# Two-layer adaLN attention kernel: 2-head exponentials in layer 0, ScalarE normalisation, and the small parts spread over each row

## The reference, cut to what matters

```python
h = layernorm(x) * (1 + ca) + sa          # "P" norm of the kernel
# layer 0: 16 heads of 8, plus one rotary part of 32 shared by all heads, causal
scores = einsum(q, k) + einsum(q_rope, k_rope)[:, None];  scores /= sqrt(40)
w = softmax(where(causal, -inf, scores));  x += ga * ((w @ v) @ W_o)
h = layernorm(x) * (1 + cb) + sb          # "T" norm
# layer 0: one shared and 15 routed experts, all computed, top 3 gated
x += gb * (shared(h) + sum_e gate_e * expert_e(h) + h)
# layer 1: the same frame; grouped qkv, 16 heads of 8, no mask
# layer 1 feed-forward: 8 experts, top 1, after one more layernorm of h ("I" norm)
```

## Time and profile before

| | us |
|---|---|
| median of 3 runs | 984.2 (981.91 to 987.36) |
| the profiled execution | 984.84 |
| its span, first to last instruction | 983.1 |
| TensorE busy | 792.4 (81%) |
| VectorE busy | 649.1 (66%) |
| ScalarE busy | 524.2 (53%) |
| GpSimd busy | 344.6 (35%) |

### The profile page before, as it was taken

How to read it: one execution, slowest core, us unless ns; L and a number is a source line. 1 busy time by engine, 2 the same in 40 slices (tenths; PEclk the granted TensorE clock), 3 DMA queues, 4 the chain that set the end, 5 groups by cost and what they waited for, 6 DMA issues and landing times. The chain is left out here.

```text
span 983.1 us, 12967 instructions
## 1 busy us (share of the span) xinstructions
PE 792.4 (81%) x4212; PEld 497.0 (51%) x4212; DVE 649.1 (66%) x1290; ACT 524.2 (53%) x970; POOL 344.6 (35%) x389
## 2 busy tenths in 40 slices
PE   3547888988898889999989899789989888527850
PEld 2233444555454667787767544345344444227740
DVE  3135568676663777776768696488898876347853
ACT  1013454545556677776757456456656656217740
POOL 3413775543532000000005345653453542133425
PEclk9987999999999999999999979899999999659985
DMA  4251331102110490000002112210110200011013
GB/s 125 48 95 21 85 81 35 34 22 46 30 24 2 137 285 6 1 1 1 1 8 57 43 42 63 60 35 17 38 25 18 58 4 10 4 54 56 32 34 84
DMA packets 56414, 44.75 MB, mean 46 GB/s; under 512 B 6598, under 2 KB 47387, under 8 KB 56347
## 3 DMA queue, kind: packets, MB, share of 16 engines
q1 hardware_dynamic: 55323, 41.82, 16.8%
q0 software_dynamic: 1024, 2.10, 0.7%
HBM read 14.67 MB, written 14.55 MB: 30 GB/s over the span
## 5 line engine op out<-in xcount | busy, mean ns | idle before, releaser
L926 ACT ACTIVATE ring<-single 128x512 f32<-128x512 f32 (+3 forms) x512 | 253.1, 517 | 226.3 <-PE single L1176 218.8
L1554 DVE TENSOR_REDUCE mneg<-pair 128x2 f32<-128x1024 f32 (+3 forms) x256 | 258.5, 1022 | 87.7 <-PE pair L1160 33.2
L1176 PE MATMUL single<-q_op,k_op 104*128 104x512 f32 (+3 forms) x512 | 216.5, 443 | 17.8 <-ACT ring L926 9.2
L1156 PE MATMUL pair<-k_op,q_op 96*128 96x512 f32 (+3 forms) x512 | 172.1, 415 | 42.2 <-DVE mneg L1554 22.6
L786 POOL TENSOR_SCALAR k_op<-k_stk,cst 104x512 fp32r<-104x512 f32 x64 | 100.0, 1577 | 276.2 <-DMA k_stk<-hl 258.5
L1176 PEld LDWEIGHTS single<-q_op,k_op 122*128 122x128 f32 (+1 forms) x512 | 97.9, 197 | 98.6 <-ACT ring L926 72.6
L1156 PEld LDWEIGHTS pair<-k_op,q_op 120*128 120x128 f32 (+1 forms) x512 | 98.9, 207 | 86.8 <-DVE mneg L1554 44.8
L1192 PE MATMUL p_o<-ring,vaug 128*9 128x512 f32 (+3 forms) x1024 | 116.1, 526 | 1.0 <-ACT ring L926 0.9
L721 POOL TENSOR_SCALAR_AFFINE_SELECT ring<-ring 128x256 f32<-128x256 f32 x128 | 52.3, 408 | 149.4 <-ACT ring L926 149.2
L955 ACT ACTIVATE ring<-pair,cols 128x512 f32<-128x512 f32 x136 | 86.1, 685 | 33.8 <-PE pair L1236 27.5
L1600 DVE TENSOR_TENSOR ring<-ring,single 128x1024 f32<-128x1024 f32 x60 | 73.3, 1221 | 45.5 <-ACT ring L955 44.4
(11 more groups left out here) (294 smaller groups left out, 1306.4 us busy)
## 6 DMA issues: line engine op xcount, KB each, us to landing
xs<-zero SPq DMA_DIRECT2D x10, 1024.0 KB, 10.1
q_op<-hl SPq DMA_DIRECT2D x96, 64.0 KB, 2.0
stage<-in_L_ffn_W_dram SPq DMA_DIRECT2D x8, 512.0 KB, 4.5
stage<-in_L_ffn_rW_dram SPq DMA_DIRECT2D x6, 512.0 KB, 5.1
k_op<-hl SPq DMA_DIRECT2D x48, 64.0 KB
k_stk<-hl SPq DMA_DIRECT2D x48, 64.0 KB, 2.0
xb<-xs SPq DMA_DIRECT2D x15, 128.0 KB, 2.0
xs<-yb SPq DMA_DIRECT2D x15, 128.0 KB, 1.7
```

Source lines behind the costliest of these rows:

```text
L926: exp_done.by(act.activation(ring[:, n % 8, lo:T], singles[n % 2][:, lo:T], ACT.Exp), (L, n))
L1156: ins = pe.matmul(both[:, i, 0:hi], r32(qs[:, P * qt:P * (qt + 1)]), r32(ks[:, 0:hi]), start=i == 0 or L == 1 or qt >= 2, stop=L == 1)
L1176: st_full.by(pe.matmul(singles[n % 2][:, lo:T], r32(ks[:, P * kc:P * (kc + 1)]), r32(qs[:, lo:T]), start=True, stop=True), (L, n))
L1554: s_taken.by(dve.tensor_reduce(mneg[:, G % 2, 2 * p:2 * p + 2, qt], both[:, :, 0:hi], axis=AX.X, op=ALU.max, negate=True), (L, m))
```

## The change

1. **Layer 0's exponentials two heads wide.** Layer 0 swaps its PSUM tiles: an exponential covers two heads (2 x 512 down to 2 x 128) in a `pair` tile, so a quad has two of them, and `max_unit` uses `single`: head pairs for query tiles 0 and 1, single heads for 2 and 3, twelve units for each group in place of eight.
2. **The parts spread over all quads** in both tables. Layer 0's `P.rs` moves from quad 4 to quad 7, the `mt` parts from "b" to "d" of quads 2, 6, 10, 14, and `rt2` and `gt` of a row come two rows later (`U.`). SyncE's list in layer 0 is not edited.
3. **The P norms of rows 1 to 3 together** (`BATCH`, new function `batch`): statistics of three rows, then one chain of Newton steps on 128x12 numbers, beside quads 0 to 3 of each layer's first row.
4. **Normalised rows by ScalarE** (`P.ne`, `T.ne`, `he`): four ACTIVATE with a pointer for bias and for scale, 128x128 each, in place of four on VectorE, which now computes only the shift (`norm_shift`).
5. **Layer 1's weight splits two to a row**, after the masks, and SyncE's loads for them at the end of the row.

```diff
-        spread = (((-5, (0, 1, 2)), (-4, (3, 4, 5)), (-3, (6, 7))), ((-6, (0, 1)), ...
+        spread = (((-5, range(0, 4)), (-4, range(4, 7)), (-3, range(7, 10)), (-2, range(10, 12))),
...
-          (2, "b"): ["mt1", "P.ne"], (2, "d"): ["T.proj"], (3, "b"): ["P.ln1", "T.ns"], (3, "d"): ["P.rp", "T.na"],
-          (4, "b"): ["T.n1"], (4, "d"): ["P.rs", "T.n2"], (5, "b"): ["ot0", "T.n3"], (5, "d"): ["P.q"],
-          (6, "b"): ["mt2", "T.ne"], (6, "d"): ["P.k"], (7, "b"): ["P.v"], (7, "d"): ["T.ln2"],
+          (4, "d"): ["P.ln1"], (5, "b"): ["ot0"], (5, "d"): ["P.rp"], (6, "b"): ["P.q"], (6, "d"): ["mt2", "T.na"], (7, "b"): ["P.rs"],
+          (8, "b"): ["P.k"], (8, "d"): ["T.n1"], (9, "b"): ["ot1", "T.n2"], (9, "d"): ["P.v"], (10, "b"): ["T.n3"], (10, "d"): ["mt3", "T.ne"],
...
+BATCH = {(0, "b"): "B.s1", (0, "d"): "B.s2", (1, "b"): "B.s3", (1, "d"): "B.sd", (2, "b"): "B.n1", (2, "d"): "B.n2", (3, "b"): "B.n3"}
...
 # SyncE, layer 1
                 m_dma(1, G + 1)
-                if r == 0:
-                    expert1(2)
-                    expert1(3)
                 m_dma(1, G + 2)
...
+                    expert1(2 * r + 2)
+                    expert1(2 * r + 3)
 # ScalarE
+                if name == "P.ne":
+                    normed.wait_ge(act, ("B.n3", L) if r else key)
...
+                    for t in range(NT):
+                        shift, scale = norm_of("P", s, t)
+                        ins = act.activation(xn[:, t, :], x[:, r, t, :], ACT.Identity, bias=shift, scale=scale)
+                    xn_ready.by(ins, key)
...
+                    at = 2 * (n % 4)
+                    ins = act.activation(ring[:, at:at + 2, lo:T], pairs[n % 2][:, :, lo:T], ACT.Exp)
 # TensorE, layer 0's quad
+                        exp_unit(L, Q, 0)
+                        for m in waiting[0:2]:
+                            max_unit(L, m)
+                        exp_unit(L, Q, 1)
+                        for name, b in beside_quad(s, q, "b"):
+                            part(name, b)
+                        for m in waiting[2:]:
+                            max_unit(L, m)
+                        if Q:
+                            values(L, Q - 1)
```

More of the change, by code:

```diff
@@ L931, in attention @@
                     Q = 4 * NG * (s % NB) + q
-                    for j in range(3):
-                        exp(L, Q, j)
+                    for i in range(NE[L] - 1):
+                        exp(L, Q, i)
                     if L and q % NT == 0 and Q:
@@ L1153, in max_unit @@
                 both = unit_scores(L, m)
-                for i in range(2):
-                    qs, ks = operands(L, G, 2 * p + i, 24)
-                    ins = pe.matmul(both[:, i, 0:hi], r32(qs[:, P * qt:P * (qt + 1)]), r32(ks[:, 0:hi]), start=i == 0 or L == 1 or qt >= 2, stop=L == 1)
+                for i, j in enumerate(heads):
+                    qs, ks = operands(L, G, j, 24)
+                    ins = pe.matmul(both[:, i, 0:hi], r32(qs[:, P * qt:P * (qt + 1)]), r32(ks[:, 0:hi]), start=i == 0 or L == 1, stop=L == 1)
                     if L == 0 and qt >= 2:
@@ L1219, in lead @@
                     max_unit(L, m)
[L1220 removed]
+                    if i == SU[L]:
                         part("mt0", NB * L)
@@ L1388, in newton, with norm_shift, batch @@
                 step(dve.scalar_tensor_tensor(out=y, in0=z, scalar=1.5, in1=y, op0=ALU.add, op1=ALU.mult))
-            def norm_end(k, src, dst):
-                for t in range(NT):
-                    ins = dve.tensor_scalar(dst[:, t, :], src[:, t, :], mv[k][:, t, 0:1], nwt[k][:, 1, t:t + 1], ALU.subtract, ALU.mult)
-                return ins
+            def norm_shift(k):
+                return dve.scalar_tensor_tensor(out=nwt[k][:, 2, :], in0=nwt[k][:, 1, :], scalar=-1.0, in1=mv[k][:, :, 0], op0=ALU.mult, op1=ALU.mult)
+            def batch(what, L):
+                v, y, z = (nwtB[:, i, :] for i in range(3))
+                if what[0] == "s" and what[1] != "d":
+                    b = int(what[1])
+                    if L == 0:
+                        dve.wait_ge(loads[4], n_load[4])
+                    elif b == 1:
+                        xn_ready.wait_ge(dve, ("P.ne", NB - 1))
+                    norm_stats("P", x[:, b, :, :])
+                    for t in range(NT):
+                        ins = dve.bn_aggr(mvB[:, NT * (b - 1) + t, :], stats["P"][:, t, :])
+                    step(ins)
+                elif what == "sd":
+                    step(dve.tensor_scalar(v, mvB[:, :, 1], EPS, None, ALU.add))
+                    step(dve.tensor_scalar(y.bitcast(I32), v.bitcast(I32), -0.5, float(0x5F3759DF), ALU.mult, ALU.add))
+                else:
+                    newton_step(v, y, z)
+                    if what == "n3":
+                        normed.by(dve.scalar_tensor_tensor(out=z, in0=y, scalar=-1.0, in1=mvB[:, :, 0], op0=ALU.mult, op1=ALU.mult), ("B.n3", L))
             def modulation():
@@ L1583, in attention @@
                     waiting = S_AT[L][4 * NG * (s % NB) + q]
-                    for m in waiting[0:1]:
+                    first = (2, 1)[L]
+                    for m in waiting[0:first]:
                         max_unit(L, m)
@@ L1587, in attention @@
                         part(name, b)
-                    for m in waiting[1:]:
+                    for m in waiting[first:]:
                         max_unit(L, m)
```

242 lines of the change are left out of this document (134 added, 108 removed), and 16 rows, old and new, of the table TABLE.

## The result

| | before | changed |
|---|---|---|
| median of 4 runs each, on the same chip | 983.06 us (980.55 to 987.36) | 1025.28 us (1018.97 to 1029.54) |
| ratio, with its 95% interval | | 1.042 (1.035 to 1.049) |
| profiled execution's span | 983.1 | 1017.2 |
| lead, up to the first exponential's matmul | 61.1 | 62.7 |
| layer 0's attention, four rows | 256.3 | 269.2 |

The account below looks back on a forecast made before the run. TensorE was taken as the busiest engine of both attentions, so only its ended waits count. Terms a to g, 26 + 4 - 23 - 9 - 7 + 10 + 3 = +4, gave 988 us for the median, range 972 to 1002.

Parts of the forecast that it names:

- d: Layer 1's first row: with weight loads moved behind the row, the 6.13 us mask wait goes; 9 us less.
- e: Layer 1: TensorE's waits for VectorE and for colliding parts shrink; 7 us less, bounds 3.4 and about 12.
- c: Layer 0: TensorE's other waits, such as those for exponentials, shrink; 23 us less, upper bound about 35.
- a: Layer 0, rows 0 to 2: copies of `mt2` queue behind SyncE's rotary transfers, so quad 8 waits; 26 us more.
- b: Layer 0: copies of the maxima come later at other quads, and GpSimd's last rope copy too; 4 us more.
- rival B: Layer 0's rows 0 to 2, quads 8 to 11: more clock loss after the queue wait; about 1000 us, chance 0.15.
- f: Layer 1: ScalarE's normalisation delays exponentials, seven blocks of 1.4 us; 10 us more, bounds 3 and 13.
- g: Serial stretches (lead, last row's parts, start of `dense`), where nothing covers `xn` or `rt2`; 3 us more.

## Why the prediction was wrong

The forecast of 988 us missed by 37. By the runs above d was off by 15 us, e by 12 to 17 and c by 10, all to the same side; a and b came out near their sizes.

**a, right.** 26 forecast, 22.7 in layer 0 by the run with the queue edited (24 in the medians); the idle time was 21.3 us against 19.5. The clock behind it cost 5.8 us by quads 7 and 8, where I took 6.3, and rival B is not needed.

**b, wrong in what it is, near in size by luck.** I had priced the later copies at 4 us (my own items add up to 4.6). In the stretch of the earlier trace rows the waits for them outside quad 8 fell from 3.8 to 2.8 us. The other half of the term was too small: the rotary copies stood at 0.3 us a row, with bounds of "0 and one copy's 1 us"; TensorE waits 1.4 to 1.6 us at quad 11 in each of three rows (the line "issue" of layer 0, 4.4 us), in all 3.4 us more. That these are the rotary copies is read from the order and from row 1, where GpSimd's last copy ends at 198.83 us and the matmul starts at 198.93; it was not tried by itself. The later place of `rs` need not be the reason: with the old places three such waits of 1.2 us are still there.

**c, too large.** 23 forecast. With the queue repaired, layer 0 was 9.8 us shorter; b's waits are 3.4 of what was given back, so c measured about 13. The waits for exponentials went, but those for `hl` fell only from 6.5 us (two kinds) to 2.2. In that run quads 0 to 8 of layer 0's second row take 32.2 us instead of 42.5, but quads 9 to 15, where the parts went, 26.7 instead of 23.3: TensorE waits there for maxima at quads 13 and 15 (0.7 and 1.2 us) and at 11 (1.4). And I gave the gain to the wide exponentials; whether they or the places gave it stays open, since the run with the old places brought the `mt` parts back to "b" as well.

**d, wrong sign: the step that failed first.** 9 us less forecast, 6 us more measured in the run with this part alone (and 5.7 in layer 1 when the rest was put back). Half of the step held: row 0 fell by 6.0 us. What I wrote of the splits was "takes the time in which GpSimd waits for the transfer anyway". I asked only who waits for GpSimd's result, not what its instruction does to another engine while it runs. In row 0 VectorE has no parts of a row before; in row 1 it has some twice as many instructions as in row 0 (x144 against x68), and a Newton step on 128x4 that meets a subtraction waits for its end. In the repaired version, where the keys' order gives row 0's share anyway, moving the splits back to row 0 was worth 12.5 us.

**e, wrong sign too.** 7 us less forecast, some 5 to 10 more measured. I counted "the collisions of parts" as gone, which is the purpose of the spread and not what its list says: in layer 1 `q` comes half a quad behind `ln1` (3.4 us for `hT`) and `ot2` half a quad behind `rk` (3.5 us for `idx`). VectorE's 6 us less work a row bought nothing, because it was seldom what TensorE waited for (3.4 us in all); that was to be read before the change.

**f, right in kind.** 10 forecast, 14 in the medians, and the waits for exponentials rose by 11.6 us. But I had placed the seven blocks in layer 1's attention, where the run with VectorE's normalisation gave 5.2 us, and the rest in the tail was g's. Where a block's price is seen by itself, the matmul waited 0.98 us and not 1.4 in the second row, and 2.2 in the first, where the batch was late.

**g.** 4 us or so in the tail by ScalarE's blocks (142.1 to 145.6 us in the three runs with them, 139.2 to 141.8 in the eight changed versions without), against my 2 to 3; but the three runs of the old lists spread from 139.1 to 142.8 us there too. The lead's 1.6 and the 2.1 of `dense` are within what the same lists differ by between executions.

The ledger by terms, from the runs: queue 24, ScalarE 14, places and GpSimd's order in layer 1 10, splits 6, the rest of layer 0 -10 (this one from a stage): 44 us, and 42 were measured. As a second test, the changed kernel less these four costs and the 18 us of the keys' order is 953 us, and the version that repairs all five was measured at 959. Its stages: 63.3, 245.5, 257.2, 253.7 and 139.6 us. That both sums come so near is partly luck, since a repair is not worth the same everywhere: the splits cost 6 us on the old kernel and 12.5 in the repaired one, the keys' order gave 18 and 4.

Open: how the 8 us between the profiled execution and the median are shared out; only its longer sisters' mean granted clock is known, 0.907 to 0.913 against 0.935. Also open is whether the batch alone helps layer 0, and what the wide exponentials are worth there; neither was tried by itself.

## What to carry to other kernels

Where work is moved between engines or places, read two lists for each moved instruction: the queue it now stands in, and the neighbours that it now meets on the shared hardware, since an instruction that nobody waits for can still hold another engine. Swapping the order of two DMA issues was worth 24 us on one kernel and 18 on the other, more than any saving of arithmetic here: ask first of each transfer which earlier entry of its queue waits longest. An engine that is busy for 60 of 69 us is still no bound when nobody waits for it; price an edit by the waits it ends.

## What was not expected of the hardware

- A VectorE step on 128x4 elements took 2.22 us instead of 0.16 beside a GpSimd subtraction of 128x1024 (2.36 us), 1.34 beside a GpSimd addition of 128x512 (1.27 us); reductions out of PSUM stayed at 1.23 us.
- A wait of TensorE of 2.12 us in a busy row was followed by a mean granted clock of 0.77 over 5 us, and one of 1.39 us, with shorter ones after it, by 0.66 and 0.50 over 5 us each; waits of 5.9 to 9.1 us by 0.67 to 0.76 over 8 us. At half speed for (1 - 0.77) x 2 = 0.46 of 5 us the first loses up to 1.2 us, the second in the same way up to 4.2, the long ones up to 1.9 to 2.6. That the second loses more in clock than its wait lasts is an upper bound; no run here varies such a wait alone.
- Four ACTIVATE with two pointers, 128x128 each, took 1.64 us together, 482 ns each.
